# Mamba stage: softplus by a maximum on VectorE, six chunks normalised by GpSimd, and two stages put earlier in their engines' orders

## The chip, the cores and the metric

The kernel runs on one core of one Trainium2 chip. The metric is the device time of one execution in microseconds (us), as the median of several runs. The engines are TensorE (PE in the profile, its weight loads PEld), VectorE (DVE), ScalarE (ACT), GpSimd (POOL) and SyncE (SP), each with a queue of its own that runs in order and meets the others at semaphores.

## The reference, cut to what matters

The input x has 4 x 512 rows of 256. The layer is a sandwich: x + 0.5 FFN(layernorm(x)), then x + mamba(layernorm(x)), then x + 0.5 FFN(layernorm(x)), where FFN is a mixture of 16 routed experts (4 for each row) and a shared one. The change lies in the middle part:

```python
xp = einsum('btd,ed->bte', x, W_in)
dt = softplus(einsum('btd,hd->bth', xp, W_dt) + b_dt)   # 32 heads of 8 channels
a  = exp(dt[..., None] * -exp(log_A))
y[t] = a[t] * y[t-1] + xp[t]                            # along the 512 rows of each batch
out = einsum('btd,ed->bte', y, W_out)
```

## The kernel before, in words

The 2048 rows are 16 tiles of 128. The first FFN runs until about 246 us of the profile, the second one from about 320 us; the Mamba stage lies between them. It works on nine chunks (line 63): chunks 0 to 6 hold two tiles (512 columns of work: two halves of 128 channels by 256 rows), chunks 7 and 8 hold one tile. The order is written out by hand: `staggered` takes, for each engine, a list of (lag, stage) and runs step s = 0 to 12; in step s each stage of the list, in the list's order, works on chunk s minus its lag. The engines' queues are strictly in that order, so a stage that waits holds up all behind it in its list. For a chunk c the work goes:

- **combine and measure** (DVE, step c, only for chunks 6 to 8; lines 1284 to 1293): the rows of the four experts are added into x (line 1148, four adds for a tile), then mean and variance. Chunks 0 to 5 were combined and measured before or at the stage's start.
- **root** (ACT, end of step c, lines 837 and 839) and four Newton steps with the shift (DVE, step c+1, lines 1187 to 1197) give the layer norm's scale and shift. For chunks 2 to 5 the roots come in steps 1 and 3, as groups of four tiles (lines 686 and 688).
- **normalise** (step c+1): on ACT (line 856) for chunks 0 to 5, on POOL (line 594) for chunks 6 to 8, of which `POOL_CHUNKS = 3` decides. GpSimd gets to it behind 16 gathers of expert rows (line 585).
- **turn** (PE, step c+1, line 1581): transposes. Then ACT's `x_in` copies them out (line 864).
- **inputs** (PE, step c+2, line 1589 by `by_channel`): xp. ACT's `xp_in` copies it (line 870).
- **step_sizes** (PE, step c+2, line 1589 again): z, the argument of softplus without its bias. It waits for `xp_in` of its own chunk.
- **logarithm** (ACT, step c+2, lines 884 to 890): relu(z + b) into m_r, |z + b|, then exp(-|.|), then ln(1 + .).
- **softplus** (DVE, step c+3, line 1314): adds the two. **decay** (ACT, step c+3, line 896): a = exp(scale x softplus), the scale being -exp(log_A) for each channel.
- **scan** (DVE, step c+3, line 1326), **outputs** (PE, step c+3, line 1614), **residual** and the next layer norm's statistics (DVE, step c+4).

The orders of one step before, with s the step:

- ACT: xp_in(s-2), decay(s-3), normalise(s-1), x_in(s-1), logarithm(s-2), root(s)
- PE: inputs(s-2), step_sizes(s-2), turn(s-1), outputs(s-3)
- DVE: softplus(s-3), first Newton step(s-1), residual(s-4), Newton steps(s-1), scan(s-3), combine(s), statistics(s-4)

At the stage's end DVE makes the scales of the next layer norm, GpSimd normalises (line 555), and the second FFN's first transposes and matmuls follow (lines 1443 and 1370).

Of the kernel before, what the change touches and what calls it, by code (L numbers as in the profile page):

```python
# [10 lines left out]
P = 128  # L11
N = B * T
NT = N // P
DC = D // P
# [50 lines left out]
POOL_CHUNKS = 3  # L65
# [18 lines left out]
def build(nc, x_d, w13r_d, w2r_d, w13s_d, w2s_d, wm_d, cst_d, hcst_d, out_d):  # L84
# [7 lines left out]
    with ctx:  # L92
# [3 lines left out]
        def sem(name):  # L96
# [14 lines left out]
                      for g in range(NE // 2)]  # L111
# [52 lines left out]
        nega = sb("nega", [P, DC])  # L164
        hid_room = sb("hid_room", [P, 4 * H])
# [45 lines left out]
        m_r = [ring_f[:, 1024 + b * 512:1024 + (b + 1) * 512] for b in range(2)]  # L211
# [92 lines left out]
                                          "abs", "relu", "exp", "log", "sp", "a", "scan", "y", "res", "neg")}  # L304
# [67 lines left out]
        def tiles(c):  # L372

            return range(*CHUNKS[c])
# [154 lines left out]
        def _(pool):  # L529
# [59 lines left out]
            def normalise(c):  # L589

                pool.wait_ge(m_s["scale"], scaled(c))
                pool.wait_ge(m_s["xt"], c - 1)
                for q, t in enumerate(tiles(c)):
                    last = pool.tensor_scalar(m_xn[c % 2][:, q, :], xres[:, t, :], rstd[:, t:t + 1], nmr[:, t:t + 1],
                                              ALU.mult, ALU.add)
                last.then_inc(m_s["xn"], 1)
# [25 lines left out]
        def _(act):  # L622
# [138 lines left out]
            for f in range(2):  # L761
# [61 lines left out]
                if f == 0:  # L823
                    act.activation(nega[:, :], cst[:, C_MB:C_MB + DC], ACT.Exp).then_inc(m_s["neg"], 1)
                    act.wait_ge(m_s["neg"], 1)
                    act.activation(nega[:, :], nega[:, :], ACT.Copy, scale=-1.0).then_inc(m_s["neg"], 1)
                    act.wait_ge(m_s["neg"], 2)

# [43 lines left out]
                    def logarithm(c):  # L872

                        b = c % 2
                        act.wait_ge(m_s["z"], c + 1)
                        if c == 1:
                            for k in range(2):
                                act.wait_ge(s_yw[k], 16 * tiles_of(k, 2))
                        if c >= 2:
                            act.wait_ge(m_s["scan"], c - 1)  # L880
                        for q in range(DC):
                            qs = part(c, q)
                            bias = cst[:, C_MB + DC + q:C_MB + DC + q + 1]
                            act.activation(m_r[b][:, qs], q_z[b][:, qs], ACT.Relu, bias=bias)
                            last = act.activation(m_t[b][:, qs], q_z[b][:, qs], ACT.Abs, bias=bias)
                        last.then_inc(m_s["abs"], 1)
                        act.wait_ge(m_s["abs"], c + 1)
                        act.activation(m_t[b][:, whole(c)], m_t[b][:, whole(c)], ACT.Exp, scale=-1.0).then_inc(m_s["exp"], 1)
                        act.wait_ge(m_s["exp"], c + 1)
                        act.activation(m_t[b][:, whole(c)], m_t[b][:, whole(c)], ACT.Ln, bias=1.0).then_inc(m_s["log"], 1)  # L890

                    def decay(c):
                        act.wait_ge(m_s["sp"], c + 1)
                        for q in range(DC):
                            qs = part(c, q)
                            last = act.activation(m_t[c % 2][:, qs], m_t[c % 2][:, qs], ACT.Exp,
                                                  scale=nega[:, q:q + 1])
                        last.then_inc(m_s["a"], 1)

                    staggered([(3, at_end(next_root, 0)), (2, xp_in), (3, decay), (1, normalise), (1, x_in), (2, logarithm), (0, root)])  # L900
# [3 lines left out]
        def _(dve):  # L904
# [316 lines left out]
            for f in range(2):  # L1221
# [52 lines left out]
                else:  # L1274
# [36 lines left out]
                    def softplus(c):  # L1311

                        dve.wait_ge(m_s["log"], c + 1)
                        dve.tensor_tensor(m_t[c % 2][:, whole(c)], m_t[c % 2][:, whole(c)], m_r[c % 2][:, whole(c)], ALU.add).then_inc(m_s["sp"], 1)
# [49 lines left out]
        def _(pe):  # L1364
# [171 lines left out]
            for f in range(2):  # L1536
# [35 lines left out]
                if f == 0:  # L1572
# [27 lines left out]
                    def step_sizes(c):  # L1600
                        pe.wait_ge(m_s["xps"], c + 1)
                        if c >= 2:
                            pe.wait_ge(m_s["abs"], c - 1)
# [15 lines left out]
                    staggered([(2, inputs), (2, step_sizes), (1, turn), (3, outputs)])  # L1619
# [53 lines left out]
```

## Time and profile before

| what | value |
|---|---|
| median of 3 runs | 573.18 us (571.89 to 574.61) |
| the profiled execution | 572.8 us, its span 571.0 us |
| granted TensorE clock, mean over the span | 0.929 of full speed |
| busy over the span: PE, DVE, ACT, POOL | 483.0, 435.0, 371.5, 352.2 us |
| the Mamba stage | about 246 to 320 us |

The profile is one execution. A row of the timeline gives start, duration, engine, line, operation, destination<-sources, form and count; in brackets the idle time of the engine before it and who ended it. Durations of instructions in a row can overlap a little, so the distance of two starts is the better measure of what one costs its engine. "bank" is PSUM, ring_f holds the softplus tiles (m_t), mamba_room the chunk buffers.

### The profile page before, as it was taken

How to read it: one execution, taken by the hardware profiler on the slowest of the kernel's cores; microseconds unless marked ns; L12 is line 12 of the kernel's file. 1: busy time of each engine (PE TensorE's matmuls, PEld its weight loads, DVE VectorE, ACT ScalarE, POOL GpSimd, SP SyncE). 2: the span in 40 equal slices, each digit the busy share in tenths (PEclk: the TensorE clock that was granted, in tenths of full speed). 3: DMA queues.
4: the chain of work that ended last, by engine and by line, in shares of the span. 5: the costliest groups of instructions: out<-in, count | busy, mean ns of one | idle time of the engine just before them, and what ended most of it. 6: DMA issues, size and time to landing. Idle time of an engine off the chain costs nothing.

```text
span 571.0 us, 13298 instructions
## 1 busy us (share of the span) xinstructions
PE 483.0 (85%) x3206; PEld 446.3 (78%) x3207; DVE 435.0 (76%) x1461; ACT 371.5 (65%) x1126; POOL 352.2 (62%) x364
## 2 busy tenths in 40 slices
PE   2969669999999999957877881469999999999784
PEld 2857459999999999836765680369999999999773
DVE  5889847777888888853598769947677888887836
ACT  2687746777777777748876464637777777776520
POOL 3699857446777777776000608077457777777774
PEclk9989579999999999979999795569999999999989
DMA  8992044656565666653000263036445555557567
GB/s 284 394 374 94 20 133 131 175 172 195 169 207 165 169 168 166 184 155 101 0 2 0 72 218 134 1 90 184 138 134 165 170 174 170 166 165 170 169 183 219
DMA packets 61149, 88.26 MB, mean 155 GB/s; under 512 B 9499, under 2 KB 46363, under 8 KB 61107
## 3 DMA queue, kind: packets, MB, share of 16 engines
q0 software_dynamic: 13728, 37.50, 25.8%
q1 hardware_dynamic: 47379, 50.29, 25.6%
q8 instruction: 15, 0.25, 0.2%
q14 instruction: 27, 0.22, 0.1%
HBM read 57.22 MB, written 30.54 MB: 154 GB/s over the span
## 4 chain that ended last, share of the span: by engine, by line
PE 57%; DVE 18%; DMA 8%; issue 6%; ACT 6%; POOL 4%; SPq 1%; POOLq 0%; ACTq 0%; DVEq 0%
PE bank L1370 27%; PE bank L1421 13%; PE bank L1391 5%; DMA ys_scratch<-ring_f 4%; PE bank L1432 3%; PE bank L1431 3%; POOL mamba_room L585 2%; PE bank L1589 1%; DVE xres L1105 1%; DVE lg L921 1%; PE bank L1614 1%; DMA ring_f<-xn_scratch,tokidx 1%; DMA raw_shared<-in_w13s 1%; DVE stage L1000 1%; DVE mamba_room L1326 1%
## 5 line engine op out<-in xcount | busy, mean ns | idle before, releaser
L1421 PE MATMUL bank<-w_routed,ring_r 128*128 x790 | 120.3, 282 | 4.3 <-DVE ring_r L951 2.8
L1421 PEld LDWEIGHTS bank<-w_routed,ring_r 128*128 128x128 f32 x790 | 109.6, 188 | 6.7 <-issue 6.7
L562 POOL DMA_INDIRECT ring_f<-xn_scratch,tokidx x80 | 77.2, 964 | 58.1 <-DVE tokidx L1082 22.4
L662 ACT ACTIVATE ring_r<-bank 128x256 fp32r<-128x256 f32 x158 | 60.8, 385 | 69.8 <-PE bank L1432 69.0
L1370 PE MATMUL bank<-w_routed,ring_r 128*128 x480 | 99.4, 343 | 0.0
L562 POOL DMA_INDIRECT ring_g<-xn_scratch,tokidx x78 | 74.5, 955 | 34.8 <-PE bank L1391 17.7
L1370 PE MATMUL bank<-w_routed,ring_x 128*128 x468 | 94.6, 337 | 0.0
L1370 PEld LDWEIGHTS bank<-w_routed,ring_r 128*128 128x128 f32 x480 | 78.0, 195 | 0.0
L1370 PEld LDWEIGHTS bank<-w_routed,ring_x 128*128 128x128 f32 x468 | 74.1, 190 | 0.0
L679 ACT ACTIVATE ring_f<-bank 128x256 f32<-128x256 f32 x158 | 60.8, 385 | 12.6 <-DMA ys_scratch<-ring_f 12.6
L949 DVE TENSOR_TENSOR ring_r<-bank,ring_r 128x128 fp32r<-128x128 f32 x158 | 45.8, 290 | 30.5 <-ACT ring_r L662 28.7
L531 POOL TENSOR_TENSOR w_routed<-raw_routed,w_routed 128x512 fp32r<-128x512 f32 (+1 forms) x38 | 55.4, 1493 | 18.9 <-ACT w_routed L638 18.8
L574 POOL DMA_INDIRECT stage<-ys_scratch,si x48 | 46.3, 965 | 15.9 <-issue 10.7
L669 ACT ACTIVATE stage<-bank 128x176 f32<-128x176 f32 x158 | 50.3, 318 | 5.2 <-PE bank L1370 5.0
L951 DVE TENSOR_TENSOR ring_r<-bank,ring_r 64x128 fp32r<-64x128 f32 x158 | 46.5, 294 | 2.1
L1370 PE MATMUL bank<-w_shared,ring_r 128*128 128x368 f32 x192 | 41.5, 359 | 4.0 <-DVE ring_r L964 4.0
L1589 PE MATMUL bank<-mamba_room,stage 128*128 128x256 f32 (+1 forms) x144 | 34.9, 389 | 11.3 <-ACT mamba_room L870 9.9
L941 DVE TENSOR_TENSOR ring_r<-bank,ring_r 128x256 fp32r<-128x256 f32 x80 | 33.9, 424 | 12.1 <-ACT ring_r L653 9.8
L1589 PEld LDWEIGHTS bank<-mamba_room,stage 128*128 128x128 f32 x144 | 26.6, 204 | 18.3 <-ACT mamba_room L870 13.1
L1391 PE MATMUL bank<-cst,ring_f 128*128 128x128 f32 x160 | 32.6, 287 | 8.6 <-DMA ring_f<-xn_scratch,tokidx 8.6
L1370 PEld LDWEIGHTS bank<-w_shared,ring_r 128*128 128x128 f32 x192 | 33.5, 201 | 5.9 <-issue 3.4
L585 POOL DMA_INDIRECT mamba_room<-ys_scratch,si x32 | 31.1, 971 | 9.8 <-issue 9.8
(188 smaller groups left out, 1070.5 us busy)
## 6 DMA issues: line engine op xcount, KB each, us to landing
ys_scratch<-ring_f SPq DMA_DIRECT2D x158, 128.0 KB
raw_routed<-in_w13r SPq DMA_DIRECT2D x6, 704.0 KB, 11.9
xn_scratch<-w_routed SPq DMA_DIRECT2D x32, 128.0 KB, 4.3
raw_routed<-in_w2r SPq DMA_DIRECT2D x6, 512.0 KB, 12.7
raw_routed<-in_w13r SPq DMA_DIRECT2D x8, 352.0 KB, 6.3
xres<-in_x_in SPq DMA_DIRECT2D x4, 512.0 KB, 7.1
raw_routed<-in_w2r SPq DMA_DIRECT2D x8, 256.0 KB, 6.8
shared_scratch<-raw_ring SPq DMA_DIRECT2D x16, 128.0 KB, 1.7
```

What stands on the lines that cost most here:

```text
L531: return pool.tensor_tensor(w_routed[0:rows, e, 1, cols], raw_routed[e // 2][0:rows, e % 2, 1, cols], w_routed[0:rows, e, 0, cols].bitcast ...
L562: pool.indirect_dma_start(xg[j % XG], None, xn_dram, bass.IndirectOffsetOnAxis(ap=tokidx[:, j:j + 1], axis=0)).then_inc(s_g[j % XG], 16)
L574: pool.indirect_dma_start(early_rows[n % ROWS], None, ys_dram[0:tiles_before(t) * P, :], bass.IndirectOffsetOnAxis(ap=si[:, n:n + 1], axis ...
L662: act.activation(hT[b][0], p_hT[b][:, 0:2 * P], ACT.Copy).then_inc(s_hhi, 1)
L669: act.activation(up[b], p_h[b][:, H:2 * H], ACT.Copy).then_inc(s_a, 1)
L679: act.activation(yb[b], p_y[b][:, 0:D], ACT.Copy).then_inc(s_yo, 1)
L949: dve.tensor_tensor(hT[b][1][:, 0:P], p_hT[b][:, 0:P], hT[b][0][:, 0:P].bitcast(f32), ALU.subtract)
L951: dve.tensor_tensor(rest, p_hT[b][64:P, P:2 * P], rest.bitcast(f32), ALU.subtract).then_inc(s_hlo, 1)
L1370: last = pe.matmul(out, a, b, start=(q == 0), stop=(q == len(terms) - 1))
L1391: last = pe.transpose(p_xT[b][:, q * P:(q + 1) * P], xg[k][:, q * P:(q + 1) * P], ident)
L1421: last = pe.matmul(p_y[b][:, 0:D], a, v, start=(q == 0), stop=(q == 4))
L1589: last = pe.matmul(out[:, part(c, e)], m_w[m][:, q * D + e * P:q * D + (e + 1) * P], src[:, part(c, q)], start=(q == 0), stop=(q == DC - 1))
```

## The change

Five edits:

1. ACT no longer makes relu(z + b). DVE's softplus is now max(z, -b) + ln(1 + exp(-|z + b|)), one `scalar_tensor_tensor` for each half, which reads z from PSUM; this is softplus(z + b) - b. The missing b is put back in the decay's exponent as a bias, -exp(log_A) x b (`shift`). ACT makes -b and the shift once, ahead of the stage, with three more instructions on 128x2 and 128x1.
2. z's bank is now read until softplus, so `step_sizes` of chunk c waits for softplus of c-2 where it waited for |.| of c-2.
3. `POOL_CHUNKS` is 6: GpSimd normalises chunks 3 to 8, ACT only 0 to 2.
4. ACT's order: decay(s-3) stands ahead of xp_in(s-2).
5. PE's order: turn(s-1) stands ahead of step_sizes(s-2).

```diff
-POOL_CHUNKS = 3
+POOL_CHUNKS = 6
...
+        negb = sb("negb", [P, DC])
+        shift = sb("shift", [P, DC])
...
                 pool.wait_ge(m_s["scale"], scaled(c))
                 pool.wait_ge(m_s["xt"], c - 1)
+                if c == NMC - POOL_CHUNKS:
+                    pool.wait_ge(m_s["xn"], c)
...
+                    act.activation(negb[:, :], cst[:, C_MB + DC:C_MB + 2 * DC], ACT.Copy, scale=-1.0).then_inc(m_s["neg"], 1)
                     act.wait_ge(m_s["neg"], 2)
+                    for q in range(DC):
+                        act.activation(shift[:, q:q + 1], cst[:, C_MB + DC + q:C_MB + DC + q + 1], ACT.Copy,
+                                       scale=nega[:, q:q + 1]).then_inc(m_s["neg"], 1)
...
-                        if c == 1:
-                            for k in range(2):
-                                act.wait_ge(s_yw[k], 16 * tiles_of(k, 2))
...
-                            act.activation(m_r[b][:, qs], q_z[b][:, qs], ACT.Relu, bias=bias)
                             last = act.activation(m_t[b][:, qs], q_z[b][:, qs], ACT.Abs, bias=bias)
...
                             last = act.activation(m_t[c % 2][:, qs], m_t[c % 2][:, qs], ACT.Exp,
-                                                  scale=nega[:, q:q + 1])
+                                                  bias=shift[:, q:q + 1], scale=nega[:, q:q + 1])
...
-                    staggered([(3, at_end(next_root, 0)), (2, xp_in), (3, decay), (1, normalise), (1, x_in), (2, logarithm), (0, root)])
+                    staggered([(3, at_end(next_root, 0)), (3, decay), (2, xp_in), (1, normalise), (1, x_in), (2, logarithm), (0, root)])
...
                         dve.wait_ge(m_s["log"], c + 1)
-                        dve.tensor_tensor(m_t[c % 2][:, whole(c)], m_t[c % 2][:, whole(c)], m_r[c % 2][:, whole(c)], ALU.add).then_inc(m_s["sp"], 1)
+                        for q in range(DC):
+                            qs = part(c, q)
+                            last = dve.scalar_tensor_tensor(m_t[c % 2][:, qs], q_z[c % 2][:, qs], negb[:, q:q + 1],
+                                                            m_t[c % 2][:, qs], ALU.max, ALU.add)
+                        last.then_inc(m_s["sp"], 1)
...
                         if c >= 2:
-                            pe.wait_ge(m_s["abs"], c - 1)
+                            pe.wait_ge(m_s["sp"], c - 1)
                         by_channel(c, q_z[c % 2], 1, m_xp).then_inc(m_s["z"], 1)
...
-                    staggered([(2, inputs), (2, step_sizes), (1, turn), (3, outputs)])
+                    staggered([(2, inputs), (1, turn), (2, step_sizes), (3, outputs)])
```

## Rows read from the trace of the kernel before

**Rows 1.** the stage: us, PE, PEld, DVE, ACT, POOL busy, TensorE clock, DMA share, GB/s

```profile
247.00:320.00 73.00, 55.97 (x246) 42.73 (x246) 46.65 (x147) 47.04 (x114) 20.87 (x26) 0.93 0.14 40
```

**Rows 2.** timeline of one regular step: start us, us, engine, line, operation

```profile
275.53 0.69 DVE L1314 TENSOR_TENSOR ring_f<-ring_f 128x512 f32<-128x512 f32 x1 [2.79 <-ACT ring_f L890]
275.91 0.60 ACT L870 ACTIVATE mamba_room<-bank 128x512 f32<-128x512 f32 x1 [0.42 <-PE bank L1589]
...
276.40 0.90 ACT L896 ACTIVATE ring_f<-ring_f,nega 128x256 f32<-128x256 f32 x2
...
276.56 1.99 PE L1589 MATMUL bank<-mamba_room,stage 128*128 128x256 f32 x8 [0.69 <-ACT mamba_room L870]
277.20 1.08 ACT L856 ACTIVATE mamba_room<-xres,nmr,rstd 128x256 f32<-128x256 f32 x2
...
279.03 0.60 ACT L864 ACTIVATE mamba_room<-bank 128x512 f32<-128x512 f32 x1 [0.75 <-PE bank L1581]
279.52 0.47 ACT L884 ACTIVATE ring_f<-bank,cst 128x256 f32<-128x256 f32 x1
279.88 0.48 ACT L885 ACTIVATE ring_f<-bank,cst 128x256 f32<-128x256 f32 x1
...
280.59 0.50 ACT L885 ACTIVATE ring_f<-bank,cst 128x256 f32<-128x256 f32 x1
281.12 0.63 ACT L888 ACTIVATE ring_f<-ring_f 128x512 f32<-128x512 f32 x1
...
282.44 0.69 DVE L1314 TENSOR_TENSOR ring_f<-ring_f 128x512 f32<-128x512 f32 x1 [3.20 <-ACT ring_f L890]
```

**Rows 3.** timeline of the stage's start

```profile
254.41 3.68 PE L1589 MATMUL bank<-mamba_room,stage 128*128 128x256 f32 x8 [2.76 <-ACT mamba_room L870]
...
259.05 0.47 ACT L884 ACTIVATE ring_f<-bank,cst 128x256 f32<-128x256 f32 x1
...
261.97 0.69 DVE L1314 TENSOR_TENSOR ring_f<-ring_f 128x512 f32<-128x512 f32 x1 [7.12 <-ACT ring_f L890]
```

**Rows 4.** timeline, GpSimd's last gather before the stage's own work

```profile
267.80 0.96 POOL L585 DMA_INDIRECT mamba_room<-ys_scratch,si  x1 [0.30 <-issue]
```

**Rows 5.** timeline of the step that turns chunk 6

```profile
285.41 3.23 DVE L1148 SCALAR_TENSOR_TENSOR xres<-mamba_room,wk,xres 128x256 f32<-128x256 f32 x8
...
287.38 1.89 PE L1589 MATMUL bank<-mamba_room,stage 128*128 128x256 f32 x8
...
290.48 0.67 DVE L1314 TENSOR_TENSOR ring_f<-ring_f 128x512 f32<-128x512 f32 x1
...
292.60 1.10 POOL L594 TENSOR_SCALAR mamba_room<-xres,rstd,nmr 128x256 f32<-128x256 f32 x2 [23.84 <-DVE nmr L1197]
...
293.75 0.66 PE L1581 MATMUL bank<-cst,mamba_room 128*128 128x128 f32 x4 [0.83 <-POOL mamba_room L594]
...
294.24 1.89 PE L1614 MATMUL bank<-stage,mamba_room 128*128 128x256 f32 x8
...
294.94 0.47 ACT L884 ACTIVATE ring_f<-bank,cst 128x256 f32<-128x256 f32 x1
...
297.86 0.69 DVE L1314 TENSOR_TENSOR ring_f<-ring_f 128x512 f32<-128x512 f32 x1 [0.72 <-ACT ring_f L890]
```

**Rows 6.** timeline of the stage's last steps

```profile
304.58 0.67 DVE L1314 TENSOR_TENSOR ring_f<-ring_f 128x512 f32<-128x512 f32 x1
...
310.09 0.42 DVE L1314 TENSOR_TENSOR ring_f<-ring_f 128x256 f32<-128x256 f32 x1 [1.70 <-ACT ring_f L890]
...
314.43 0.43 DVE L1314 TENSOR_TENSOR ring_f<-ring_f 128x256 f32<-128x256 f32 x1
...
316.52 2.07 PE L1614 MATMUL bank<-stage,mamba_room 128*128 128x256 f32 x4 [2.77 <-DVE mamba_room L1326]
```

**Rows 7.** TensorE by stretch: us, busy (x matmuls), granted clock, DMA share, GB/s

```profile
254.40:257.60 3.20, 3.19 (x8) 0.52 0.44 126
```

**Rows 8.** groups of instructions by line in 247 to 322 us: count, busy us, mean ns

```profile
L1148 DVE SCALAR_TENSOR_TENSOR xres<-mamba_room,wk,xres 128x256 f32<-128x256 f32 x16 | 7.1, 475 | 0.2
```

More of the change, by code:

```diff
@@ L210, in build @@
         m_t = [ring_f[:, b * 512:(b + 1) * 512] for b in range(2)]
-        m_r = [ring_f[:, 1024 + b * 512:1024 + (b + 1) * 512] for b in range(2)]
         pb = [ctx.enter_context(nc.psum_tensor(f"bank{i}", [P, 512], f32)) for i in range(8)]
@@ L303, in build @@
         m_s = {n: sem("m_" + n) for n in ("var2", "ln2", "r02", "scale2", "var", "ln", "r0", "scale", "xn", "xt", "xin", "xp", "xps", "z",
-                                          "abs", "relu", "exp", "log", "sp", "a", "scan", "y", "res", "neg")}
+                                          "abs", "exp", "log", "sp", "a", "scan", "y", "res", "neg")}
         def tiles_of(k, ring):
@@ L892, in decay @@
                     def decay(c):
+                        if c == 0:
+                            act.wait_ge(m_s["neg"], 3 + DC)
                         act.wait_ge(m_s["sp"], c + 1)
@@ L1311, in softplus @@
                     def softplus(c):
+                        if c == 0:
+                            dve.wait_ge(m_s["neg"], 3)
                         dve.wait_ge(m_s["log"], c + 1)
-                        dve.tensor_tensor(m_t[c % 2][:, whole(c)], m_t[c % 2][:, whole(c)], m_r[c % 2][:, whole(c)], ALU.add).then_inc(m_s["sp"], 1)
+                        for q in range(DC):
[3 more added lines that the diff above has]
+                        last.then_inc(m_s["sp"], 1)
                     def scan(c):
```

## The prediction

> **What bounds the kernel now.** I took the windows by stage first. The change touches only the 73 us between the two FFNs [rows 1], so only they can move. No engine is full there: PE is busy 56.0 of 73, ACT 47.0, DVE 46.7. The stage is bound by a loop through the engines, and the timeline of one step shows it [rows 2]. I mark time by S(c), the start of softplus of chunk c on DVE (line 1314). From S(2) = 275.53 to S(3) = 282.44 it goes: ACT copies xp (275.91), PE makes z (276.56 to 278.55), ACT in the meantime does decay (276.40) and normalise (277.20 to 278.28), waits 0.75 us for the turn, copies it (279.03), and only then starts the logarithm at 279.52, 0.97 us after z was there. ACT's own list is what the step is made of: 6.9 us with little idle time in it.
>
> From chunk 6 on another path joins: softplus(4) at 290.48, behind it on DVE the Newton steps, then GpSimd's normalise at 292.60, the turn at 293.75, the copy, logarithm(5) at 294.94, softplus(5) at 297.86 [rows 5]. z(5) is no part of it: PE ran it at 290.92, before the turn. The last steps take 6.72, 5.51 and 4.34 us [rows 5, 6].
>
> **The change part by part.**
>
> *Relu gone.* Four PSUM passes at distances of 0.36 us [rows 2] become two: 279.52 to 281.12 was 1.60, the new pair 0.36 + 0.53 = 0.89 (the last one's distance is 281.12 - 280.59). With exp and ln (281.12 to 282.44, 1.32) the logarithm takes 2.21 instead of 2.92: 0.71 less.
>
> *Softplus on DVE.* No row has this form. Below, it costs the 0.69 of the add that it replaces [rows 2]; above, two adds of the scalar_tensor_tensor form on 256 columns: eight in a row took 3.23, 0.40 each [rows 5], and the last is out after its mean of 0.475 [rows 8], so 0.88. I take 0.85, nearer the row of the same opcode and width. That is 0.15 to 0.2 more at each chunk. The page VectorE: DVE Perf Modes of the Trainium skill (section on the TRN2 errata) says that each instruction pays a fixed latency, so two halves pay it twice, and gives a larger one for PSUM sources than for SBUF. By its cycle table two halves from PSUM would be 0.78, an estimate.
>
> *Three small ACT instructions* before the first chunk delay it by about 0.7 us. I cost them at nothing: what follows waits for DVE's variances anyway and z(0) starts only at 254.41, after PE had been idle for 2.76 us [rows 3]. Without that cover they cost their 0.7.
>
> *Decay ahead of xp_in.* It puts softplus and decay into the loop of z: softplus 0.85, decay 0.80 (276.40 to 277.20), xp_in 0.65 (275.91 to 276.56), z 1.99, logarithm 2.21, four handovers of about 0.03: **6.6 us**. The step before was 6.8 on average ((282.44 - 261.97)/3) [rows 2, 3]. So the Relu's gain is mostly spent: 0.2 is left in each step where nothing else binds, although ACT itself would be far from full.
>
> *Turn ahead of step_sizes.* z(s-2) now waits on PE for the normalising of s-1. While ACT still normalises (chunk 2, in step 3) this adds 1.08 for the normalise and 0.49 for the turn (293.75 to 294.24, [rows 5]) in place of ACT's idle: the step from S(0) to S(1) is 6.6 + 1.5 = 8.1. S(0) comes sooner: the logarithm starts as before near 259.05 [rows 3], since the turn, now first, delays z(0) by about what the copy no longer does; with 2.21 for it S(0) = 261.3, 0.7 earlier. Sum up to S(3): -0.7 + (8.1 + 2 x 6.6 - 20.47) = +0.1.
>
> *GpSimd's three more chunks.* It is in the gathers until 268.76 [rows 4]; normalise takes 1.10 for two tiles [rows 5], so chunk 3 is ready at 269.9. In the new schedule S(1) is 269.4 and the z(2) behind the turn of chunk 3 cannot start before S(1) + 0.85 + 0.80 + 0.65 = 271.7, so this hides, by 1.3 us. If it comes later than 271.2 the turn blocks PE. The instructions are off ACT, but ACT's time was no longer the bound; worth nothing more.
>
> The Trainium skill, SBUF — State Buffer, "SBUF: two separate sides", speaks against this part: VectorE operations with two SBUF inputs and GpSimd exclude each other for whole instructions. By that, GpSimd's pair could start up to one VectorE instruction late, which rows already hold: its pair at 292.60 took 1.10 beside VectorE's work.
>
> *Chunk 6.* The step of the eight adds is DVE's own list, 8.04 from S(3) to S(4) [rows 2, 5], plus 0.2 for softplus: 8.2. Then PE, in its new order, holds step_sizes(5) until the turn of chunk 6. Before, turn to S(5) was 4.11 (293.75 to 297.86); now it is turn 0.49, z 1.99, logarithm 2.21, handovers 0.1 = 4.8. With softplus 0.2 longer ahead of the Newton steps this step takes 7.38 + 0.7 + 0.15 = 8.2. The same again for chunk 7 (z(6) is still full width): +0.75. Chunk 8 goes with the half-size z(7): +0.4. Last step +0.05. Sum: 0.1 + 0.2 + 0.85 + 0.75 + 0.4 + 0.05 = **+2.35**.
>
> *The clock.* PE before was idle 1.65 us between inputs(5), which end at 289.27, and z(5) at 290.92 [rows 5]. In the new order nothing is on PE between inputs(5), done near 289.4, and the turn at 290.48 + 0.3 + 0.2 + 3.27 = 294.25: 4.8 us idle. The rows show what shorter pauses did: after 2.76 us z(0) ran at half clock (1.2 of 2.4 GHz), 3.68 us for what takes 1.99 [rows 2, 3, 7]; after 2.77 us the last outputs did too, four matmuls in 2.07 [rows 6]. Turn and z(5) at the lower level cost up to 0.49 + 1.69 more, on the path. I take **2.0**; ends 0 and, with a second fall of the same size ahead of the turn of chunk 7 or 8, 4.2. That the array's clock falls when idle and comes back only with activity is also what TensorE: Matmul & The Clock Gate of the Trainium skill says ("the default state is throttled, and activity releases the throttle", Part 1); the rows agree.
>
> *Sum.* +2.35 + 2.0 and 0.15 for the last softplus = **+4.5**. On the profiled execution: 572.8 + 4.5 = 577.3 (its span 571.0 to 575.5). It lies 0.4 below the median of the runs, so in the median 573.18 + 4.5 = **577.7 us**.
>
> **The rivals.**
>
> *Relief of ACT decides: faster.* Edit 3 takes 1.08 from three steps of ACT, edit 1 takes 0.71 from nine. If the loop through decay does not bind, because softplus, which DVE is idle for (3.20 us [rows 2]), comes early enough, a step would fall to PE's list: three groups of 8 matmuls at 1.89 [rows 5] and the turn 0.49, 6.2. That is 0.6 in each of eight steps and 0.7 from S(0), 5.5 in all: 567.7. For it: PE was only waiting for ACT. Against it: the loop is a sum of durations in the rows, and turn(6) is behind DVE whatever ACT does. It decides if S(1)-S(2) is under 6.3.
>
> *The clock holds: slower by a little.* Only +2.5, 575.7. For it: the pause of 1.65 us left the clock full; against it: the pause grows to 4.8.
>
> *Gain and loss cancel.* z(0) escapes the half clock, since inputs(0) end later with the three small instructions and the turn goes first: up to 1.0 from S(0), and softplus costs 0.69: nine times 0.16, 1.4. With the clock's 2.0 the sum is +2.1, without it 0: 573 to 575.3.
>
> *Late GpSimd: slower still.* If its normalises are late for chunks 3 to 5 too, the turn ahead of z stalls three more steps by about 1 each: 580.7.
>
> **How the numbers follow.** Forecast with the clock loss 0.50 (575.5 to 580); clock holds 0.14; cancel 0.15; relief 0.13; late GpSimd 0.08. A measurement of this kernel can tell about 0.5%, 2.9 us, from no change, so slower means above 576.05 and faster below 570.3. Slower: 0.48 of the forecast, 0.08 late, 0.06 of the others: 0.62. Faster: 0.12. Same: 0.26. Range: leaving out most of the relief case below and the double clock loss with late GpSimd above, 572 to 581.
>
> **What would show it.** S(c) again from the softplus rows: S(0)-S(1) about 8.1, then 6.6 and 6.6; the turn of chunk 6 directly ahead of z(5) on PE, with an idle time near 4.8 us before it and a clock of 0.5 behind it; S(4)-S(5) near 10; softplus pair 0.8 to 0.9; hidden matmuls of the second FFN (line 1370) at 325 instead of 320.5. Wrong if the steps between chunks 1 and 3 fall to 6.2, or if the turns of chunks 6 to 8 come sooner after softplus than 3.3 us.

## The result, and the profile after

The changed kernel takes **580.54 us** (median of 6 runs, 578.25 to 581.52), the kernel before 573.61 (6 runs, 568.82 to 574.89) beside it. The ratio of the times is 1.0132, with a 95% interval of 1.0100 to 1.0163: slower by 7.6 us. (The ratios here are taken over all the runs and are not quotients of the medians; the two medians differ by 6.9 us.) I had forecast 577.7, +4.5. So it is slower, as forecast and inside the range, but by more than the sum gave, and one term of the sum, the clock's, is most of the reason.

| | before | after |
|---|---|---|
| profiled execution, its span | 572.8, 571.0 us | 580.4, 578.6 us |
| granted TensorE clock, mean | 0.929 | 0.913 |
| busy: PE, DVE, ACT, POOL | 483.0, 435.0, 371.5, 352.2 | 489.9, 436.7, 366.1, 354.8 us |
| first hidden matmul of the second FFN | 320.50 | 328.49 us |

ACT does less, as meant, and PE is busier though it has no more to do. The second matters. The prediction marked time by S(c), the start of softplus of chunk c on DVE; the same marks in the profile of after:

| | S(0) | S0-S1 | S1-S2 | S2-S3 | S3-S4 | S4-S5 | S5-S6 | S6-S7 | S7-S8 | sum |
|---|---|---|---|---|---|---|---|---|---|---|
| before | 261.97 | 6.78 | 6.78 | 6.91 | 8.04 | 7.38 | 6.72 | 5.51 | 4.34 | 52.46 |
| forecast, clock full | 261.3 | 8.1 | 6.6 | 6.6 | 8.2 | 8.2 | 7.5 | 5.9 | 4.4 | 55.5 |
| after | 261.00 | 10.34 | 6.76 | 6.77 | 8.41 | 9.74 | 7.29 | 6.13 | 5.62 | 61.06 |

Three steps stand out: the first, the fifth and the last. TensorE by stretch in the profile of after (us; then busy time and count of PE, PEld, DVE, ACT and POOL; granted clock; DMA share; GB/s), the pause ahead of chunk 6 and what follows it, and two more stretches like it:

```profile
264.50:268.90 4.40, 4.32 (x13) 3.61 (x13) 0.00 (x0) 0.62 (x2) 3.45 (x5) 0.50 0.33 96
292.90:296.70 3.80, 0.00 (x0) 0.00 (x0) 3.70 (x13) 1.82 (x5) 1.09 (x2) 1.00 0.00 0
296.70:300.60 3.90, 3.88 (x12) 3.23 (x13) 3.21 (x9) 0.60 (x1) 0.00 (x0) 0.56 0.02 6
313.20:317.90 4.70, 4.69 (x20) 4.10 (x21) 1.74 (x5) 2.66 (x7) 0.00 (x0) 0.64 0.00 0
```

Between 292.90 and 296.70 us no matmul runs, and the next 3.9 us have a mean clock of 0.56. I had forecast that. I had not forecast the first and the last row: 0.50 behind the turn of chunk 2, and 0.64 from the turn of chunk 8 on. The timeline of after shows how they come about, first in the stretch from S(0) to S(2), which answers to [rows 2, 3]:

```profile
261.00 0.88 DVE L1323 SCALAR_TENSOR_TENSOR ring_f<-bank,negb,ring_f 128x256 f32<-128x256 f32 x2 [6.46 <-ACT ring_f L893]
...
263.44 1.08 ACT L863 ACTIVATE mamba_room<-xres,nmr,rstd 128x256 f32<-128x256 f32 x2
...
264.58 1.11 PE L1592 MATMUL bank<-cst,mamba_room 128*128 128x128 f32 x4 [3.71 <-ACT mamba_room L863]
...
265.49 3.62 PE L1600 MATMUL bank<-mamba_room,stage 128*128 128x256 f32 x8
...
268.46 1.09 POOL L597 TENSOR_SCALAR mamba_room<-xres,rstd,nmr 128x256 f32<-128x256 f32 x2
...
271.34 0.88 DVE L1323 SCALAR_TENSOR_TENSOR ring_f<-bank,negb,ring_f 128x256 f32<-128x256 f32 x2 [6.98 <-ACT ring_f L893]
...
272.25 1.09 ACT L901 ACTIVATE ring_f<-ring_f,shift,nega 128x256 f32<-128x256 f32 x2 [0.61 <-DVE ring_f L1323]
...
273.25 0.57 ACT L877 ACTIVATE mamba_room<-bank 128x512 f32<-128x512 f32 x1
...
273.88 1.99 PE L1600 MATMUL bank<-mamba_room,stage 128*128 128x256 f32 x8 [0.52 <-ACT mamba_room L877]
...
275.91 0.84 ACT L888 ACTIVATE ring_f<-bank,cst 128x256 f32<-128x256 f32 x2 [1.60 <-PE bank L1600]
...
278.10 0.88 DVE L1323 SCALAR_TENSOR_TENSOR ring_f<-bank,negb,ring_f 128x256 f32<-128x256 f32 x2 [2.59 <-ACT ring_f L893]
```

Line numbers have moved by 1 to 11: the turn is line 1592, inputs and step_sizes 1600, outputs 1625, softplus 1323, normalise 863 (ACT) and 597 (POOL). The turn of chunk 2 waits until ACT has normalised that chunk behind decay and xp_in; PE has by then stood still for 3.71 us. z(1) behind it takes 3.62 us instead of 1.99. The regular step follows: softplus 271.34, decay 272.25, xp_in 273.25, z 273.88, |.| 275.91, next softplus 278.10. That is the loop I had written down, in its order.

The step that turns chunk 6, answering to [rows 5], and the stage's end, answering to [rows 6], in the timeline of after:

```profile
293.28 0.86 DVE L1323 SCALAR_TENSOR_TENSOR ring_f<-bank,negb,ring_f 128x256 f32<-128x256 f32 x2
...
295.57 1.09 POOL L597 TENSOR_SCALAR mamba_room<-xres,rstd,nmr 128x256 f32<-128x256 f32 x2 [19.75 <-DVE nmr L1202]
...
296.72 0.87 PE L1592 MATMUL bank<-cst,mamba_room 128*128 128x128 f32 x4 [3.87 <-POOL mamba_room L597]
...
297.39 3.40 PE L1600 MATMUL bank<-mamba_room,stage 128*128 128x256 f32 x8
...
313.21 0.44 PE L1592 MATMUL bank<-cst,mamba_room 128*128 128x128 f32 x2 [2.51 <-POOL mamba_room L597]
...
314.64 3.31 PE L1625 MATMUL bank<-stage,mamba_room 128*128 128x256 f32 x8
...
324.52 2.07 PE L1625 MATMUL bank<-stage,mamba_room 128*128 128x256 f32 x4 [3.19 <-DVE mamba_room L1337]
```

z(5) is now on the path from turn to softplus(5) and costs 3.40 us of it. Ahead of the turn of chunk 8 PE stands still for 2.51 us, and outputs(6) behind it take 3.31 instead of 1.89. The four last outputs run at half clock as they did before [rows 6].

### The profile page after: what moved, and what is told of

It reads as the page before. It is cut to its first block, busy times and chain, and to the rows that moved or that the text cites. A ratio compares the mean times of both kernels' runs of the same rounds, so it can differ in the third digit from the quotient of the medians.

```text
span 578.6 us, 13292 instructions
## 1 busy us (share of the span) xinstructions
PE 489.9 (85%) x3206; PEld 453.2 (78%) x3207; DVE 436.7 (75%) x1470; ACT 366.1 (63%) x1105; POOL 354.8 (61%) x370
## 4 chain that ended last, share of the span: by engine, by line
PE 61%; DVE 11%; issue 9%; DMA 7%; ACT 7%; POOL 3%; SPq 1%; POOLq 0%; ACTq 0%; DVEq 0%
PE bank L1381 28%; PE bank L1432 13%; PE bank L1402 5%; DMA ys_scratch<-ring_f 4%; PE bank L1489 3%; PE bank L1443 2%; PE bank L1442 2%; PE bank L1600 2%; POOL mamba_room L586 2%; DVE xres L1110 1%; PE bank L1625 1%; PE bank L1454 1%; DMA raw_shared<-in_w13s 1%; DVE stage L1005 1%; DVE ring_f L1076 1%
## 5 line engine op out<-in xcount | busy, mean ns | idle before, releaser
L1600 PE MATMUL bank<-mamba_room,stage 128*128 128x256 f32 (+1 forms) x144 | 38.1, 418 | 3.4 <-ACT mamba_room L877 2.8
L575 POOL DMA_INDIRECT raw_shared<-ys_scratch,si x32 | 30.8, 963 | 9.8 <-issue 7.9
L1600 PEld LDWEIGHTS bank<-mamba_room,stage 128*128 128x128 f32 x144 | 29.4, 224 | 9.0 <-ACT mamba_room L877 3.7
```

The source lines that it names most:

```text
L575: pool.indirect_dma_start(early_rows[n % ROWS], None, ys_dram[0:tiles_before(t) * P, :], bass.IndirectOffsetOnAxis(ap=si[:, n:n + 1], axis ...
L1600: last = pe.matmul(out[:, part(c, e)], m_w[m][:, q * D + e * P:q * D + (e + 1) * P], src[:, part(c, q)], start=(q == 0), stop=(q == DC - 1))
```

## The experiments

In all of them S(c) is read from the profile and the ratio from timed runs beside the kernel before (its medians were 572.35, 573.02 and 572.35 us in the three series). One profile is one execution, and its span holds differences that lie outside the steps: the second FFN, from the first hidden matmul to the end, took between 249.5 and 252.6 us in these profiles, and S(0) came between 258.9 and 262.6. So the steps tell the mechanism and the ratio the size, and where the two disagree the text says so.

| kernel | S0-S1 | S1-S2 | S2-S3 | S3-S4 | S4-S5 | S5-S6 | S6-S7 | S7-S8 | sum | median | ratio |
|---|---|---|---|---|---|---|---|---|---|---|---|
| after | 10.34 | 6.76 | 6.77 | 8.41 | 9.74 | 7.29 | 6.13 | 5.62 | 61.06 | 580.54 | 1.0132 |
| pe_order_back | 9.43 | 7.68 | 7.69 | 8.41 | 7.67 | 7.33 | 6.35 | 4.86 | 59.42 | 579.84 | 1.0126 |
| act_order_back | 9.20 | 6.35 | 6.80 | 9.79 | 10.19 | 8.34 | 5.80 | 4.93 | 61.40 | 584.12 | 1.0199 |
| both_orders_back | 6.47 | 7.22 | 6.57 | 8.87 | 6.82 | 7.14 | 5.19 | 5.01 | 53.29 | 572.92 | 1.0019 |
| keep_pe_awake | 9.11 | 6.77 | 6.76 | 8.41 | 10.01 | 7.56 | 6.98 | 4.59 | 60.19 | 581.19 | 1.0162 |
| before_turn_first | 10.15 | 9.15 | 9.98 | 9.99 | 10.31 | 8.98 | 6.15 | 4.25 | 68.96 | 589.74 | 1.0269 |
| awake_shorter | 8.19 | 6.76 | 6.77 | 8.42 | 8.04 | 7.30 | 5.82 | 4.59 | 55.89 | 576.16 | 1.0059 |
| before_softplus_only | 6.48 | 6.76 | 6.80 | 8.75 | 6.82 | 7.15 | 5.18 | 5.02 | 52.96 | 572.81 | 0.9991 |
| before_six_chunks | 6.77 | 6.93 | 7.49 | 8.04 | 7.36 | 6.72 | 5.51 | 4.34 | 53.16 | 572.65 | 0.9995 |
| orders_where_early | 6.47 | 9.78 | 6.76 | 8.41 | 6.81 | 7.15 | 5.43 | 6.01 | 56.82 | 574.19 | 1.0035 |
| both_back_awake | 6.48 | 7.11 | 6.57 | 8.86 | 6.81 | 7.14 | 5.44 | 5.99 | 54.40 | 571.71 | 0.9982 |
| before_awake | 6.81 | 6.78 | 6.92 | 8.05 | 7.37 | 6.72 | 5.52 | 4.34 | 52.51 | 569.84 | 0.9953 |
| best_of_all | 6.47 | 8.43 | 6.76 | 7.75 | 6.82 | 6.49 | 5.23 | 6.66 | 54.61 | 572.50 | 0.9995 |

### The two orders, one at a time and together

**pe_order_back**: only ACT's new order is left.

```diff
-                    staggered([(2, inputs), (1, turn), (2, step_sizes), (3, outputs)])
+                    staggered([(2, inputs), (2, step_sizes), (1, turn), (3, outputs)])
```

> The changed kernel with only TensorE's order put back (step sizes ahead of the turn). Theory A, the turn ahead of the step sizes costs by putting z behind GpSimd's and ScalarE's normalising and by the pauses that drop the clock: the step from S(4) to S(5) falls from 9.7 to about 7 us, S(0) to S(1) from 10.3 to 8, but each regular step grows from 6.8 to 7.8, because the copy of the turn now stands ahead of the logarithm while decay still stands ahead of the copy of xp; all in all 2 to 3 us faster than the changed kernel, 577.5. Theory B, ScalarE's order is the cost and TensorE's is not: no gain at all, 580.

Measured: ratio 1.0126 [1.0097 to 1.0156], no better than the whole change. The time is what theory B said, the steps are what theory A said. S4-S5 fell from 9.74 to 7.67, so the turn ahead of step_sizes is what cost chunk 6's step; but the regular steps went up from 6.76 to 7.68. The steps add up to 1.6 us less than in the change; in this one profile the second FFN took 1.9 us more (252.0 for 250.1), and the time is the same. One of the regular steps in its timeline:

```profile
271.82 1.09 ACT L901 ACTIVATE ring_f<-ring_f,shift,nega 128x256 f32<-128x256 f32 x2 [0.61 <-DVE ring_f L1323]
...
272.82 0.57 ACT L877 ACTIVATE mamba_room<-bank 128x512 f32<-128x512 f32 x1
...
273.44 1.99 PE L1600 MATMUL bank<-mamba_room,stage 128*128 128x256 f32 x8 [1.80 <-ACT mamba_room L877]
...
275.27 0.60 PE L1592 MATMUL bank<-cst,mamba_room 128*128 128x128 f32 x4
...
275.91 0.60 ACT L871 ACTIVATE mamba_room<-bank 128x512 f32<-128x512 f32 x1 [2.52 <-PE bank L1592]
```

Decay holds up xp_in and z as in the change, but now the turn stands behind z on PE, and x_in (line 871) and the logarithm behind it on ACT. ACT waits 2.52 us for that turn. Turn first had been what kept x_in out of this loop.

**act_order_back**: only PE's new order is left.

```diff
-(3, decay), (2, xp_in), (1, normalise), (1, x_in), (2, logarithm), (0, root)])
+(2, xp_in), (3, decay), (1, normalise), (1, x_in), (2, logarithm), (0, root)])
```

> The changed kernel with only ScalarE's order put back (copy of xp ahead of decay). Theory A (loop through softplus and decay, 6.8 us a step, goes away): the two steps with GpSimd's chunks, S(1) to S(3), fall to about 6.1 each and the last ones by 1 or more, the steps with the pauses stay (10 and 9.7): 3 to 4 us faster than the changed kernel, 577. Rival (decay is hidden, only TensorE's order matters): within 0.5 us of the changed kernel, 580.

Measured: ratio 1.0199 [1.0165 to 1.0232], 584.12 us. Both readings missed: taking ACT's new order alone out of the change makes it 3.6 us worse. What the stage loses lies between S(3) and S(6), where the three steps are 2.9 us longer; the other steps are 2.5 shorter, so the sum of the steps is up by 0.3 only. In this profile the second FFN took 252.6 us for 250.1; what makes the rest of the 3.6 us is not shown. The loss in the stage, in the timeline:

```profile
283.92 0.88 DVE L1323 SCALAR_TENSOR_TENSOR ring_f<-bank,negb,ring_f 128x256 f32<-128x256 f32 x2 [1.36 <-ACT ring_f L893]
...
285.72 0.60 ACT L877 ACTIVATE mamba_room<-bank 128x512 f32<-128x512 f32 x1 [1.84 <-PE bank L1600]
286.22 1.08 ACT L901 ACTIVATE ring_f<-ring_f,shift,nega 128x256 f32<-128x256 f32 x2
...
287.33 1.39 DVE L1337 TENSOR_TENSOR_SCAN mamba_room<-ring_f,mamba_room,bank 128x256 f32<-128x256 f32 x2 [1.94 <-ACT ring_f L901]
```

Softplus(3) is early, but ACT's next instruction is xp_in (line 877), which waits for PE's inputs until 285.72. Decay stands behind it, and so the scan starts 3.41 us after softplus (2.03 in the change, 286.90 after 284.87), DVE's adds for chunk 6 behind the scan, and with them the turn of chunk 6, ahead of which PE now stands still for 4.66 us.

**both_orders_back**: both diffs above, so the old orders with the new softplus and the six chunks.

> The changed kernel with both orders put back; what is left of the change is softplus on VectorE from PSUM and GpSimd's six chunks. If the orders are the whole loss: regular steps of 6.55 us (TensorE's list), S(4) to S(5) at 6.8, no pause of TensorE over 2.8 us in the stage, 2 us faster than the kernel before, 571.5. If softplus on VectorE or GpSimd's chunks cost something themselves: as the kernel before or slower, 573 to 575.

Measured: ratio 1.0019 [0.9999 to 1.0040], 572.92 us, between the two expectations. The loss of the change is in the two orders, and of the other edits together no cost or gain can be told. The table of ratios, old and new order of each engine, all with the new softplus:

| | step_sizes first (old) | turn first (new) |
|---|---|---|
| xp_in first (old) | 1.0019 | 1.0199 |
| decay first (new) | 1.0126 | 1.0132 |

Each order alone costs: ACT's 6.1 us, PE's 10.3. PE's order on top of ACT's costs nothing that can be told, and ACT's on top of PE's gives back 3.8. They don't add; the rows above show why, since each moves the wait that the other stands behind.

**before_turn_first**: the kernel before, with PE's new order alone.

```diff
-                    staggered([(2, inputs), (2, step_sizes), (1, turn), (3, outputs)])
+                    staggered([(2, inputs), (1, turn), (2, step_sizes), (3, outputs)])
```

> The kernel before with TensorE's new order alone (turn ahead of step sizes). If the turn's place costs by itself: with ScalarE's normalising in front of the turn in chunks 1 to 5, regular steps of 7.9 instead of 6.8 us, the turn of chunk 6 behind VectorE and ahead of z(5), S(4) to S(5) 8.7 or, with a fall of the clock, 10 or more; time 581 to 584. If the place only matters together with decay's: no change, 573.

Measured: ratio 1.0269 [1.0236 to 1.0303], 589.74 us, beyond what either reading said. In its timeline the turns of chunks 1 to 5 all wait for ACT's normalise, as I had said of chunk 2 alone:

```profile
275.29 1.08 ACT L856 ACTIVATE mamba_room<-xres,nmr,rstd 128x256 f32<-128x256 f32 x2
...
276.43 0.66 PE L1581 MATMUL bank<-cst,mamba_room 128*128 128x128 f32 x4 [2.46 <-ACT mamba_room L856]
```

PE stands still for 2.46 to 3.24 us ahead of these turns, and they take up to 1.11 us for the 0.66 of the full clock; the mean clock from 250 to 320 us is 0.78. In the change the turns of chunks 3 to 5 find their input ready, so GpSimd's three more chunks, worth nothing in the old order, look like what makes turn first bearable. No run has these two edits alone, so this is argued and not shown.

### The two edits that are left

**before_softplus_only**: both_orders_back with three chunks on GpSimd, so that only the new softplus and decay are left (edits 1 and 2).

```diff
-POOL_CHUNKS = 6
+POOL_CHUNKS = 3
```

> The kernel before with the new softplus (maximum on VectorE, shift in decay) alone: old orders, three chunks on GpSimd. Regular steps 6.5 instead of 6.8 us, since ScalarE's list is 0.7 shorter and TensorE's, 6.55, binds; the steps from S(3) to S(6), where VectorE's list binds, 0.5 to 1 us longer in all by the longer softplus and the later scan; within 0.5 us of the kernel before. If reading PSUM and the bias slow anything else: slower by over 1 us.

Measured: ratio 0.9991 [0.9967 to 1.0015]. The Relu's 0.71 us a step buys nothing that can be told. The timeline shows who takes them:

```profile
273.95 0.88 DVE L1323 SCALAR_TENSOR_TENSOR ring_f<-bank,negb,ring_f 128x256 f32<-128x256 f32 x2 [2.35 <-ACT ring_f L893]
...
274.77 0.60 ACT L877 ACTIVATE mamba_room<-bank 128x512 f32<-128x512 f32 x1 [0.85 <-PE bank L1600]
275.26 1.08 ACT L901 ACTIVATE ring_f<-ring_f,shift,nega 128x256 f32<-128x256 f32 x2
```

ACT comes to xp_in sooner and waits 0.85 us for PE's inputs, where it waited 0.42 [rows 2]; decay takes 0.98 where it took 0.80. From S(3) to S(4) the step is even 0.7 longer: the scan of chunk 3 waits for that later and longer decay and starts 2.38 us after softplus (283.13 after 280.75) where it took 1.67 (284.11 after 282.44), and DVE's adds stand behind it.

**before_six_chunks**: the kernel before with six chunks on GpSimd.

```diff
-POOL_CHUNKS = 3
+POOL_CHUNKS = 6
...
+                if c == NMC - POOL_CHUNKS:
+                    pool.wait_ge(m_s["xn"], c)
```

> The kernel before with six chunks on GpSimd alone. ScalarE loses 1.1 us in each of steps 4 to 6, but the turn stays behind z on TensorE and the copy of it ahead of the logarithm: 6.6 instead of 6.8 us a step, within 0.6 us of the kernel before. If GpSimd is late behind its gathers, S(2) to S(3) is over 7 us.

Measured: ratio 0.9995 [0.9971 to 1.0020]; S2-S3 is 7.49 for 6.91 and S1-S2 6.93 for 6.78, the rest as before. A step over 7 was to mean a late GpSimd, but the turn of chunk 3 stands directly behind z(2) (268.74) and waits for nothing. What does differ is VectorE: its small instructions beside GpSimd's normalises take longer (last section). In that step ACT waits 1.00 us for PE's inputs and 1.73 for the turn, where it waited 0.42 and 0.75 [rows 2]: its waits for PE grow by 1.56, more than the 1.08 us that were taken off it.

### The clock by itself

If the falls of the clock are the missing term, work on PE in the pauses must take it away without touching an order. The added matmuls multiply data that lies in SBUF, and a bank of PSUM that the turn overwrites takes their result, which nobody reads.

**keep_pe_awake**: the changed kernel, with 12 such calls ahead of the turn of chunk 2, 14 ahead of chunk 6, 5 and 9 ahead of 7 and 8.

```diff
+                        for k in range({2: 12, 6: 14, 7: 5, 8: 9}.get(c, 0)):
+                            pe.matmul(q_xT[c % 2][:, 0:256], ident, m_w[0][:, 0:256], start=True, stop=True)
                         pe.wait_ge(m_s["xn"], c + 1)
```

> The changed kernel with matmuls added whose results are overwritten, ahead of the turns of chunks 2, 6, 7 and 8 (12, 14, 5 and 9 of 256 columns), in TensorE's pauses. If the clock's falls cost what the rows say (1.9 at S(0) to S(1), 1.7 at S(4) to S(5), 1.2 at S(7) to S(8)): those steps fall to 8.2 to 8.5, 8.1 and 4.5 us and the time by 4 to 5, to 576. If the pauses' waits are the loss and the clock is not: no change, or slower by what the added matmuls stand in the way.

Measured: ratio 1.0162 [1.0129 to 1.0194], a miss by too large a dose. The clock was full throughout (1.00 from 261 to 320 us), but a call takes 0.43 us, and the turn now waits for the calls, in the timeline:

```profile
295.90 1.10 POOL L597 TENSOR_SCALAR mamba_room<-xres,rstd,nmr 128x256 f32<-128x256 f32 x2 [19.74 <-DVE nmr L1202]
...
299.06 0.60 PE L1594 MATMUL bank<-cst,mamba_room 128*128 128x128 f32 x4
```

GpSimd was done at 297.00 and the turn started at 299.06. So the run shows that the clock can be held, and not what it is worth.

**awake_shorter**: the same with fewer calls.

```diff
-                        for k in range({2: 12, 6: 14, 7: 5, 8: 9}.get(c, 0)):
+                        for k in range({2: 7, 6: 8, 7: 3, 8: 4}.get(c, 0)):
```

> The changed kernel with fewer matmuls in TensorE's pauses (7, 8, 3 and 4 ahead of the turns of chunks 2, 6, 7 and 8; keep_pe_awake had so many that the turns started up to 2 us late). If the clock's falls are a part of the loss: full clock from 262 us to the last outputs, steps S(0) to S(1) 8.4, S(4) to S(5) 8.1, S(7) to S(8) 4.6, together 4 us less than in the changed kernel, 576. If not: 580.

Measured: ratio **1.0059** [1.0031 to 1.0087], 576.16 us. First the stage by stretch (columns as above), then the timeline at the turns of chunks 2 and 6:

```profile
261.00:320.00 59.00, 50.60 (x253) 42.74 (x251) 39.36 (x119) 35.63 (x80) 11.87 (x17) 1.00 0.06 18
```

```profile
266.06 0.66 PE L1594 MATMUL bank<-cst,mamba_room 128*128 128x128 f32 x4 [1.02 <-ACT mamba_room L863]
...
266.55 1.89 PE L1602 MATMUL bank<-mamba_room,stage 128*128 128x256 f32 x8
...
296.05 0.66 PE L1594 MATMUL bank<-cst,mamba_room 128*128 128x128 f32 x4 [0.41 <-POOL mamba_room L597]
...
296.54 1.89 PE L1602 MATMUL bank<-mamba_room,stage 128*128 128x256 f32 x8
```

The clock is full over the stage (0.88 in the change), the turns wait for their data and not for the calls, and z behind them takes 1.89 us for 3.62 and 3.40. Nothing else in the kernel differs from the change, and its steps fall to what I had forecast with the clock full: 55.89 in sum against 55.5. So of the change's +7.6 us, 1.0132 - 1.0059 or about **4.2 us** are the clock's falls, and about 3.4 are the waits that are left. By the two intervals the 4.2 is known to some 2.4 us either way (an estimate); the steps of the two profiles give 5.2. One profile's span would not have shown it: the profiled run of awake_shorter was its slowest, 578.62, with a second FFN of 252.3 us.

### What can be kept of the change, and of the clock

**orders_where_early**: turn first only for chunks 3 to 5, decay first only for chunks 1 to 3, old orders elsewhere.

```diff
+                    first = lambda stage, want: lambda c: stage(c) if (1 <= c < 4) == want else None
+                    staggered([(3, at_end(next_root, 0)), (3, first(decay, True)), (2, xp_in), (3, first(decay, False)), (1, normalise), (1, x_in), (2, logarithm), (0, root)])
...
+                    early = lambda stage, want: lambda c: stage(c) if (3 <= c < 6) == want else None
+                    staggered([(2, inputs), (1, early(turn, True)), (2, step_sizes), (1, early(turn, False)), (3, outputs)])
```

> The changed kernel with the new orders only in steps 4 to 6: the turn ahead of z for chunks 3 to 5, which GpSimd has normalised early, decay ahead of the copy of xp for chunks 1 to 3; the old orders elsewhere. If the new places cost only where what they wait for is late: no pause of TensorE over 2 us ahead of the turns of chunks 2, 6, 7 and 8, steps 6.5, 6.8, 6.8, 8.4, 6.8, 7.1, 5.2 and 5.0, sum 52.6, as both_orders_back or 0.5 us faster, 572.5. If they cost by themselves: 575 or more.

Measured: ratio 1.0035 [1.0011 to 1.0058], slower than the old orders. S1-S2 is 9.78, and its timeline shows why:

```profile
268.16 3.23 POOL L597 TENSOR_SCALAR mamba_room<-xres,rstd,nmr 128x256 f32<-128x256 f32 x6
...
269.30 0.73 PE L1593 MATMUL bank<-cst,mamba_room 128*128 128x128 f32 x4 [2.74 <-POOL mamba_room L597]
...
269.82 3.54 PE L1601 MATMUL bank<-mamba_room,stage 128*128 128x256 f32 x8
```

GpSimd leaves its gathers at 268.1 as ever, but S(1) is at 265.82 and not at 271.34. The turn of chunk 3 stands still for it 2.74 us, the clock falls, and z(2) takes 3.54 for 1.89. This is my rival of a late GpSimd, which the change itself escapes only because its own first step is late.

**both_back_awake** and **before_awake**: both_orders_back, and the kernel before, with three calls after inputs(0) and six ahead of the last outputs.

```diff
+                        for k in range(3 if c == 0 else 0):
+                            pe.matmul(q_xT[0][:, 0:256], ident, m_w[0][:, 0:256], start=True, stop=True)
...
+                        for k in range(6 if c == NMC - 1 else 0):
+                            pe.matmul(q_xT[0][:, 0:256], ident, m_w[0][:, 0:256], start=True, stop=True)
```

> both_orders_back with 3 matmuls added behind inputs(0) and 6 ahead of outputs(8), where TensorE idles 1.8 to 3.1 us; their results are overwritten or unused. If a fall of the clock is what these pauses cost: full clock for z(0) in every run and 2.07 to 1.2 us for the last outputs, the second FFN's first hidden matmuls 1.3 instead of 2.0 us; 1.5 to 2.5 us faster than both_orders_back, 570.5 to 571.5. Rival: the clock falls again before the second FFN, no change, 572.9.

> The kernel before with the same added matmuls. As for both_back_awake: 1.5 to 2.5 us faster than the kernel before if the clock's falls at the stage's two ends are on the path, no change if they are not.

Measured: 0.9982 [0.9960 to 1.0003] and **0.9953** [0.9933 to 0.9973]. The second, 569.84 us, is faster than the kernel before by 2.7 us and than the change by about 10. Its timeline of TensorE where [rows 3, 6] had the half clock:

```profile
253.76 1.99 PE L1589 MATMUL bank<-mamba_room,stage 128*128 128x256 f32 x8 [0.52 <-ACT mamba_room L870]
...
314.24 1.13 PE L1618 MATMUL bank<-stage,mamba_room 128*128 128x256 f32 x4 [0.17 <-DVE mamba_room L1326]
...
317.63 1.27 PE L1370 MATMUL bank<-w_shared,ring_r 128*128 128x368 f32 x6
```

z(0) takes 1.99 for 3.68 and the last outputs 1.13 for 2.07; the mean clock from 250 to 320 us is 0.99. (One profile shows little of this: in that of before_six_chunks z(0) took 1.99 and the last outputs 1.13 without added calls. The ratio, over all runs, is what counts.) The first hidden matmul comes 5.48 us after S(8) at 312.15, where it came 6.07 after (320.50 after 314.43).

**best_of_all**: orders_where_early with those calls, and the next layer norm's statistics of chunks 2 and 4 done with those of chunk 5.

```diff
+                        if c in (2, 4):
+                            return
...
-                        for t in tiles(c):
-                            last = statistics(t)
+                        for n in (2, 4, 5) if c == 5 else (c,):
+                            for t in tiles(n):
+                                last = statistics(t)
```

> orders_where_early with the added matmuls of both_back_awake and VectorE's statistics of chunks 2 and 4 moved from the steps that VectorE's list binds to step 9. S(3) to S(4) 7.7 instead of 8.4, S(5) to S(6) 6.6 instead of 7.1, S(6) to S(7) up to 0.3 longer: about 1 us faster than both_back_awake, 569.5 to 570.5, faster than both kernels. If VectorE's list does not bind there, as both_back_awake.

Measured: ratio 0.9995 [0.9966 to 1.0025]. The moved statistics gave what they should where DVE binds, S3-S4 7.75 for 8.41 and S5-S6 6.49 for 7.15. S1-S2 kept the stall on GpSimd (8.43), and S7-S8 went to 6.66, where outputs(6) ran at half clock, 3.66 us for 1.89 (the row is shown in the last section). No gain is left.

## Why the prediction was right and where it failed

The direction and the path were right: slower, with the turn ahead of z and a fall of the clock behind the pause at chunk 6. The sum was too small, 4.5 for 7.6, and the step that failed is the size of its clock term.

**Clock**, the step that failed: "I take 2.0", one fall, at chunk 6. There were three: at the turns of chunks 2, 6 and 8, after pauses of 3.71, 3.87 and 2.51 us. Against awake_shorter they cost 2.15, 1.70 and 1.34 us (the last two steps together), 5.2 in the profile and 4.2 in the timed runs. That is the upper end of the term, 4.2, or beyond it; I had kept that end for one more fall at chunk 7 or 8. (Two falls of my own 0.49 + 1.69 would have been 4.4.) The fall at chunk 2 was to be had from my own numbers. I had written that z(1) would wait for normalise and turn, 1.5 us over and above a loop of 6.6, and never asked how long PE would stand still there, though I asked it for chunk 6. With its 2.15 the sum would have been +6.65.

**Regular step**, 6.6: measured 6.76. The loop is the one named. The missing 0.16 is mostly decay: its pair has a pointer bias besides its pointer scale now, and takes 1.09 and a distance of 1.00 to the next instruction (272.25 to 273.25), for which I had kept the 0.80 of before. The Trainium skill says so, ScalarE: Activation LUTs, "What ACT_TABLE_LOAD costs": each pointer operand adds some 93 ns to an activation. Two of them are 0.19, the trace agrees with 0.20, and I had costed the edit at nothing without asking. Softplus, forecast 0.85, took 0.88 (and 0.79 until DVE's next instruction). The logarithm took 2.19 (275.91 to 278.10) for 2.21.

**First step**, 8.1 with full clock: 8.19 in awake_shorter, 10.34 in the change.

**Chunk 6**: full-clock forecast 8.2, measured 8.04 in awake_shorter. The pause was forecast at 4.8 and was 3.87, because PE's inputs(5) ended only at 292.85, later against S(4) than I had put them; the turn came 3.44 us after S(4) for 3.77. S5-S6 7.30 for 7.5, S6-S7 5.82 for 5.9, S7-S8 4.59 for 4.4.

**Edits at nothing**: S(0) was 261.00 for 261.3, so nothing speaks against the three small instructions of ACT being hidden; but S(0) scatters by 3.7 us between the profiles, with these instructions or without, and one profile can't price them. GpSimd's chunk 3 was normalised at 269.55, 0.35 before my 269.9, and hid.

**Rivals**: relief of ACT is refuted in both parts (before_softplus_only, before_six_chunks). That the clock holds is refuted by the windows; its argument, the pause ahead of z(5) in the kernel before, stands in this row of that kernel's timeline:

```profile
290.92 1.99 PE L1589 MATMUL bank<-mamba_room,stage 128*128 128x256 f32 x8 [1.65 <-ACT mamba_room L870]
```

Cancelling did not happen in the change; without its two orders gain and loss do cancel (both_orders_back). Late GpSimd did not happen in the change and did in orders_where_early. With the clock held the change is 3.4 us slower (1.8 to 5.0 by its interval), against the 2.5 that I had without the clock.

Why both_orders_back gains nothing although ACT has less to do, its timeline of DVE shows, in the step from S(3) = 279.14 to S(4) = 288.01 (8.87 for 8.04):

```profile
281.63 1.39 DVE L1337 TENSOR_TENSOR_SCAN mamba_room<-ring_f,mamba_room,bank 128x256 f32<-128x256 f32 x2 [1.02 <-ACT ring_f L901]
```

The scan waits 1.02 us for decay and starts 2.49 us after softplus, where it was 1.67 in the kernel before; from the scan to the next softplus both take the same, 6.38 and 6.37. That is the 0.83 by which the step is longer. The next step is 0.56 shorter (6.82 for 7.38), since DVE no longer waits for the logarithm there.

What stays open is where the rest of act_order_back's loss lies. Nor was GpSimd started earlier by fewer gathers ahead of it, which orders_where_early would need.

## What to carry to other kernels

An engine whose list is in order gives everything behind a stage that stage's wait: before moving one forward, write down what it waits for in every phase of the loop, here with ACT, with GpSimd behind its gathers, and with the chunks that DVE has still to prepare. Then take each pause of TensorE that the new order makes and price the clock's fall behind it as a term of its own. Where a pause can't be closed, a few matmuls without a reader close it, if they end before the data comes.

## What the runs showed of the hardware

The fall of the clock doesn't always stand where one looks for it. After 2.76 us idle z(0) began at half clock in the kernel before [rows 3]. After 2.77 us the turn at 255.07 of the change took 0.66 us, the full clock, and only then did the clock fall, under the matmuls of z(0) and inputs(1). Ahead of the turn of chunk 8 it was the same. TensorE by stretch of after (us; busy time and count of PE; granted clock; DMA share; GB/s):

```profile
255.00:256.00 1.00, 0.93 (x7) 1.00 0.44 131
256.00:257.00 1.00, 1.00 (x4) 0.53 0.35 102
313.20:314.20 1.00, 0.99 (x8) 0.94 0.00 0
314.20:315.20 1.00, 1.00 (x6) 0.50 0.00 0
```

PE is busy in all four rows, and the level goes from 1.00 to 0.50 nearly 1 us after work had begun again. The half level is 1.2 GHz, and the loss then falls on the matmuls behind the ones that ended the pause. And a pause can be short. In both_back_awake, timeline of TensorE:

```profile
305.61 0.69 PE L1592 MATMUL bank<-cst,mamba_room 128*128 128x128 f32 x2 [1.50 <-POOL mamba_room L597]
306.14 3.22 PE L1629 MATMUL bank<-stage,mamba_room 128*128 128x256 f32 x8
```

After 1.50 us idle the turn of two matmuls took 0.69 us (0.44 in the change), and outputs(6) behind it 3.22 for 1.89. In the change a pause of 1.67 us ahead of the turn of chunk 7 did nothing: 0.44, and z(6) in 1.89. Three more pairs say the same. In before_turn_first three turns each came after exactly 2.46 us idle; z behind the first took 1.89 us, and behind the other two 3.29 and 3.54. The last outputs of the kernel before came after 2.77 us at half clock; in before_six_chunks, in the same place, they came after 2.76 us at the full one. And in best_of_all 0.86 us idle stood ahead of a turn at full clock (305.59), with outputs(6) at half clock behind it:

```profile
314.39 1.13 PE L1616 MATMUL bank<-stage,mamba_room 128*128 128x256 f32 x4 [2.76 <-DVE mamba_room L1328]
...
306.12 3.66 PE L1633 MATMUL bank<-stage,mamba_room 128*128 128x256 f32 x8
```

The first row is from before_six_chunks, the second from best_of_all. Against that, 3.32 us idle ahead of the turn of chunk 8 in act_order_back (315.12) left the clock full: 0.44, and outputs(6) in 1.89. So the length of the pause just ahead doesn't say whether it costs; the range of the term has to start at nothing and go up to the whole difference. The Trainium skill, TensorE: Matmul & The Clock Gate, Part 1, says of the rise of the clock that its point varies from run to run; these rows show such scatter for its falls.

The prediction weighed whether VectorE and GpSimd shut each other out. An effect of this kind does show in the rows, but it is VectorE that is held up. In before_six_chunks, where GpSimd normalises from 267.60 on:

```profile
267.58 0.61 DVE L1195 TENSOR_SCALAR hid_room<-hid_room 128x4 f32<-128x4 f32 x1
```

The same instruction takes 0.17 us in the kernel before (270.22), with GpSimd idle. In the change, four such instructions from 329.24 on took 0.48 to 0.51 us each beside GpSimd's next normalises, and GpSimd's own stayed at 0.54. In the Mamba stage of the change the Newton steps (272.13 to 273.55) ran ahead of GpSimd's pair of chunks (273.65), so they cost nothing there.

More calls in a pause are not better: 40 of them in the changed kernel gave 1.0162 and 22 gave 1.0059, where it has 1.0132 without any. The best number between them was not sought.
